# A patch-and-text Mamba layer with a shared and a routed FFN on one core: the four engines' work behind the last scan is put in another order

## The reference, cut to what matters

```python
h = concat([cls, patches(x) @ W + b], axis=1) + pos_enc         # 64 sequences
h = concat([h, txt], axis=1)                                    # 114 tokens of 256
h = h + mamba(layernorm(h))            # in-proj, conv, silu, selective scan, y * silu(z) @ W_out
def moe(v):                            # v = layernorm(h)
    sh  = ln(silu(v @ sw1.T + sb1) * (v @ sw2.T + sb2)) @ sw3.T + sb3
    xm  = v[index_b, index_t]                       # 512 chosen rows
    s   = sigmoid(xm @ [sg_w; eg_w].T + bias)       # 1 shared score, 8 expert scores
    top = argmax(s[:, 1:] + exp_bias);  w = softmax([s[:, 0], s[:, 1:][top]])
    z   = ln(silu(xm @ ew1 + eb1) * (xm @ ew2 + eb2))          # all 8 experts, hidden 128
    e   = (z @ ew3 + eb3)[top]
    sh[index_b, index_t] = sh[index_b, index_t] * w[0] + e * w[1]
    return sh
out = h + moe(layernorm(h))
```

## Time and profile before

| | before |
|---|---|
| median of three runs | 1710.02 us (1707.89 to 1710.78) |
| the profiled execution | 1707.03 us, of which the span is 1704.8 us |
| busy: PE, DVE, ACT, POOL | 87%, 90%, 78%, 92% of the span |
| last scan ends, last combine begins | 1619.58 us, 1700.00 us |
| granted TensorE clock over the span | 0.948 of full |

### The profile page before, as it was taken

The page is one execution under the profiler, slowest core; times in us unless marked ns, Lnnn a source line. Parts: engine busy times, 40 slices in busy tenths (PEclk is TensorE's granted clock), DMA queues, the critical chain, the costliest instruction groups (busy, mean ns, idle before and its releaser), DMA issues.

```text
span 1704.8 us, 27981 instructions
## 1 busy us (share of the span) xinstructions
PE 1485.8 (87%) x9868; PEld 1062.9 (62%) x9868; DVE 1539.9 (90%) x1360; ACT 1322.1 (78%) x3071; POOL 1562.6 (92%) x782
## 2 busy tenths in 40 slices
PE   7778898898998988988989889899898898987688
PEld 7555666666666666666666666666666666654355
DVE  2599999999999999999999999999999999998944
ACT  2577888888888888888888888888888888886644
POOL 0699999999999999999999999999999999999914
PEclk9898999999999999999999999999999999997799
DMA  5667665555666555556665555566655565656110
GB/s 142 141 135 183 166 139 124 125 128 132 147 131 148 136 123 125 131 131 145 133 148 134 125 123 132 133 144 133 148 134 123 124 132 133 139 125 140 40 35 16
DMA packets 194430, 218.47 MB, mean 128 GB/s; under 512 B 94011, under 2 KB 184773, under 8 KB 193778
## 3 DMA queue, kind: packets, MB, share of 16 engines
q1 hardware_dynamic: 193522, 215.51, 55.4%
q0 software_dynamic: 576, 1.17, 0.3%
q10 hardware_dynamic: 192, 0.01, 0.0%
HBM read 169.92 MB, written 47.09 MB: 127 GB/s over the span
## 4 chain that ended last, share of the span: by engine, by line
DVE 27%; POOL 25%; PE 16%; ACT 15%; issue 10%; DMA 5%; SPq 1%; DVEq 0%; ACTq 0%; POOLq 0%
POOL xr L1757 16%; DVE psum L1375 13%; ACT psum L1046 7%; DVE xr L1384 7%; DVE xr L1375 5%; POOL xr L1765 5%; PE psum L624 4%; POOL u L1778 3%; DMA u<-u_scratch 3%; PE psum L725 2%; ACT L1077 2%; PE psum L796 2%; ACT soft L1094 2%; PE psum L797 2%; ACT soft L1098 1%
## 5 line engine op out<-in xcount | busy, mean ns | idle before, releaser
L1757 POOL TENSOR_TENSOR xr<-u,bbc 128x912 f32<-128x912 f32 x512 | 1075.6, 2132 | 13.6 <-DMA u<-u_scratch 13.6
L1046 ACT ACTIVATE psum<-delta,a_neg 128x228 f32<-128x228 f32 x2048 | 804.9, 441 | 209.1 <-DVE xr L1384 178.8
L1375 DVE TENSOR_TENSOR_SCAN psum<-psum,xr 128x912 f32<-128x912 f32 x320 | 655.1, 2047 | 14.3 <-POOL xr L1757 8.4
L1765 POOL TENSOR_TENSOR xr<-xr,cbc 128x912 f32<-128x912 f32 x192 | 408.3, 2126 | 32.5 <-DVE xr L1375 32.3
L1375 DVE TENSOR_TENSOR_SCAN xr<-psum,xr 128x912 f32<-128x912 f32 x192 | 393.1, 2047 | 19.1 <-ACT psum L1046 19.1
L1384 DVE TENSOR_TENSOR xr<-psum,cbc 128x912 f32<-128x912 f32 x320 | 352.3, 1101 | 4.8
L725 PE MATMUL psum<-xr,fold 128*32 128x228 f32 x4096 | 297.4, 388 | 27.5 <-DVE xr L1384 14.7
L624 PE MATMUL psum<-xh,win 128*128 128x228 f32 x1024 | 220.3, 364 | 30.9 <-ACT xs L1077 24.9
L624 PEld LDWEIGHTS psum<-xh,win 128*128 128x128 f32 x1024 | 190.8, 191 | 57.4 <-ACT xs L1077 35.0
L675 PE MATMUL psum<-xi,conv_d 128*128 128x228 f32 x1024 | 211.4, 358 | 0.0
L675 PEld LDWEIGHTS psum<-xi,conv_d 128*128 128x128 f32 x1024 | 190.9, 189 | 16.4 <-issue 11.7
(11 more groups left out here) (207 smaller groups left out, 1550.1 us busy)
## 6 DMA issues: line engine op xcount, KB each, us to landing
delta<-delta_scratch SPq DMA_DIRECT2D x256, 228.0 KB, 6.6
u<-u_scratch SPq DMA_DIRECT2D x256, 228.0 KB, 4.3
bbc<-bc_scratch SPq DMA_DIRECT2D x128, 114.0 KB, 2.5
u_scratch<-u SPq DMA_DIRECT2D x64, 228.0 KB, 3.6
cbc<-bc_scratch SPq DMA_DIRECT2D x128, 114.0 KB, 2.7
delta_scratch<-delta SPq DMA_DIRECT2D x64, 226.0 KB, 5.6
out<-ob SPq DMA_DIRECT2D x32, 228.0 KB
h_scratch<-h SPq DMA_DIRECT2D x31, 228.0 KB
```

The source lines that it names most:

```text
L1046: ins = nc.scalar.activation(slot(k)[:, j * TOK:(j + 1) * TOK], delta4[:, c // 2, j, c % 2], ACT.Exp, scale=a_neg[:, c, j, n:n + 1])
L1375: nc.vector.tensor_tensor_scan(x if k in on_pool(i) else slot(k), slot(k), x, 0.0, ALU.mult, ALU.add).then_inc(scan_done, 1)
L1757: nc.gpsimd.tensor_tensor(xr[:, k % XRING], u4[:, c // 2, :, c % 2], bbc[:, p, n].unsqueeze(1).to_broadcast([P, J, TOK]), ALU.mult).then_i ...
L1765: nc.gpsimd.tensor_tensor(xr[:, k % XRING], xr[:, k % XRING], cbc[:, p, k % NI].unsqueeze(1).to_broadcast([P, J, TOK]), ALU.mult).then_inc ...
```

## The change

It touches the tail and the end of the body of group 31, and nothing before. (1) The last output projection is split: `out_first` (both identity parts and the first two of four wout chunks) stands in group 31's body, where bias_rows was; `out_second` (the other two chunks) opens the tail. Its PSUM bank is CB and no longer AB. (2) bias_rows moves into the tail and into bank 0. (3) The last FFN group uses bank BB and no longer 3, and its output leaves through xs and no longer through ob, so hidden(0, 1) waits for the copy of group 30 and not for that of 31. (4) All four engines' tails are written in another order. (5) SP no longer waits between the last two output DMAs.

```diff
-            h2_ps = psum[0:T, AB, 0:SEQ * DM].rearrange("p (s d) -> p s d", s=SEQ)
+            def h2_ps(g):
+                return psum[0:T, CB if g == GROUPS - 1 else AB, 0:SEQ * DM].rearrange("p (s d) -> p s d", s=SEQ)
+            def ob_of(g):
+                if g == GROUPS - 1:
+                    return xs[:, (GROUPS - 2) % 2].rearrange("p c t -> p (c t)")[:, 0:SEQ * DM].rearrange("p (s d) -> p s d", s=SEQ)
+                return ob[:]
...
-                return {GROUPS - 2: 2, GROUPS - 1: 3}.get(g, AB)
+                return {GROUPS - 2: 2, GROUPS - 1: BB}.get(g, AB)
...
-                        sp.dma_start(out_groups[g], ob[0:T]).then_inc(out_out, 16)
-                        sp.wait_ge(out_out, 16 * (g + 1))
+                        sp.dma_start(out_groups[g], ob_of(g)[0:T]).then_inc(out_out, 16)
...
+                    def out_first():
+                        g = GROUPS - 1
+                        pe.wait_ge(sz_done, 2 * GROUPS)
+                        pe.wait_ge(y_done, CH // 2 * g + 1)
+                        for s in range(SEQ):
+                            for k in range(DC):
+                                pe.matmul(h2_ps(g)[:, s, k * P:(k + 1) * P], h0[:, g % HRING, k, s * T:(s + 1) * T], ident[:],
+                                          start=(s == 0 and k == 0), stop=False)
+                            for c in range(CH // 2):
+                                pe.matmul(h2_ps(g)[:, s], y[:, g % 2, c, s * T:(s + 1) * T], wout[:, c], start=False, stop=False)
+                    def out_second():
+                        g = GROUPS - 1
+                        pe.wait_ge(y_done, CH // 2 * GROUPS)
+                        for s in range(SEQ):
+                            for c in range(CH // 2, CH):
+                                mm = pe.matmul(h2_ps(g)[:, s], y[:, g % 2, c, s * T:(s + 1) * T], wout[:, c],
+                                               start=False, stop=(s == SEQ - 1 and c == CH - 1))
+                        mm.then_inc(h2_mm, 1)
...
+                        if runs(i):
+                            reduce_states(i, 13)
                         if i == GROUPS - 1:
-                            bias_rows()
-                        if runs(i):
-                            reduce_states(i, 13)
+                            out_first()
...
                     def hidden(m, j):
+                        pe.wait_ge(xmt_ev, m + 1)
                         if m >= 1:
                             pe.wait_ge(a_done, 2 * m - 1 + j)
                         elif j == 0:
-                            pe.wait_ge(scan_done, UNITS * GROUPS)
-                            pe.wait_ge(c_dve, ALL_DVE)
+                            pe.wait_ge(eb3_done, 1)
                         else:
-                            pe.wait_ge(o_done, GROUPS)
+                            pe.wait_ge(o_done, GROUPS - 1)
...
                     def out_copy(g):
                         act.wait_ge(f3_mm, g + 1)
-                        need(act, out_out, 16 * g)
-                        nc.scalar.activation(ob[0:T], f3_ps(g), ACT.Copy).then_inc(o_done, 1)
+                        if g == GROUPS - 1:
+                            act.wait_ge(h2_mm, GROUPS)
+                        else:
+                            need(act, out_out, 16 * g)
+                        nc.scalar.activation(ob_of(g)[0:T], f3_ps(g), ACT.Copy).then_inc(o_done, 1)
...
-                    turn_out(0)
                     hidden(3, 0)
+                    turn_out(0)
                     hidden(3, 1)
-                    for m in range(1, MT):
-                        turn_out(m)
-                        expert_out(m - 1)
-                    expert_out(MT - 1)
+                    turn_out(1)
+                    expert_out(0)
+                    turn_out(2)
+                    expert_out(1)
+                    expert_out(2)
+                    turn_out(3)
+                    expert_out(3)
```

More of the change, by code:

```diff
@@ L997, in expert_out @@
                         mm.then_inc(e3_mm, 1)
-                    pe.wait_ge(gw_in, GW_IN)
-                    v_center(ga)
-                    h2_turn(gz)
-                    v_var(ga)
-                    ffn_in(gz)
+                    out_second()
+                    v_center(GROUPS - 3)
+                    h2_turn(GROUPS - 2)
+                    v_var(GROUPS - 3)
+                    ffn_in(GROUPS - 2)
+                    bias_rows()
+                    v_center(GROUPS - 2)
+                    h2_turn(GROUPS - 1)
+                    ffn_out(GROUPS - 3)
+                    v_var(GROUPS - 2)
                     turn_rows(0)
-                    ffn_out(ga)
-                    v_center(gz)
+                    ffn_in(GROUPS - 1)
                     turn_rows(1)
                     hidden(0, 0)
-                    v_var(gz)
                     turn_rows(2)
+                    ffn_out(GROUPS - 2)
                     turn_rows(3)
-                    ffn_out(gz)
-                    for m in range(MT):
-                        gates(m)
+                    gates(0)
+                    gates(1)
+                    gates(2)
+                    v_center(GROUPS - 1)
+                    gates(3)
                     hidden(0, 1)
+                    v_var(GROUPS - 1)
                     hidden(1, 0)
@@ new lines, in gate_weights, with hot_copy @@
+                    def gate_weights():
+                        act.wait_ge(gate_step, GATE_STEPS - 3)
+                        nc.scalar.activation(wts[:], two[:], ACT.Exp).then_inc(gate_act, 1)
+                    def hot_copy():
+                        act.wait_ge(hot_mm, 1)
+                        nc.scalar.activation(hot_t.rearrange("p m t -> p (m t)"), psum[0:E, CB, :], ACT.Copy).then_inc(hot_ev, 1)
+                    ln2_rstd(GROUPS - 2)
+                    h2_scale(GROUPS - 2)
+                    h2_copy(GROUPS - 1)
@@ L1351, in _ @@
[L1351 to L1352 removed]
+                    out_copy(GROUPS - 2)
+                    gate_scores()
+                    v_square(GROUPS - 1)
+                    ln3_rstd(GROUPS - 1)
+                    gate_weights()
                     gate_silu(0)
[L1354 to L1355 removed]
@@ L1356, in _ @@
                     gate_silu(1)
+                    out_copy(GROUPS - 1)
                     affine(0)
+                    hot_copy()
                     gate_silu(2)
+                    affine(1)
                     zt_copy(0)
-                    affine(1)
                     gate_silu(3)
-                    for m in range(1, MT):
-                        zt_copy(m)
-                        if m + 1 < MT:
-                            affine(m + 1)
+                    affine(2)
+                    zt_copy(1)
@@ L1367, in _ @@
+                    zt_copy(2)
+                    affine(3)
+                    zt_copy(3)
                 @block.vector
@@ L1544, in body @@
                             scan(i, 15)
-                        if runs(i - 2) and not in_window(i - 2):
+                        if i < GROUPS - 1 and runs(i - 2) and not in_window(i - 2):
                             ffn_first(i - 2)
```

204 lines of the change are left out of this document (100 added, 104 removed).

## The result

The changed kernel has a median of 1699.98 us over five runs (1697.99 to 1701.16), the kernel before 1710.01 us over five runs beside them (1707.89 to 1710.78). The ratio is 0.9942, with an interval from 0.9929 to 0.9954: 10.0 us less.

The account below looks back on a forecast made before the run. The prediction took a latency chain, then PE's queue, to bound the tail. Head 4.2 us and second part 1.1 us shorter made 5.3 us less, a median of 1704.7 us (-0.31%), range 1700.5 to 1708.5.

Parts of the forecast that it names:

- the old tail's price (61.4): PE's time from the first turn_rows to the last expert_out's end in the old profile: 61.4 us, 56.74 busy.
- the rival of the clock: PE's granted clock falls in the new, denser tail: slower, 2.5 to 7.5 us lost, up to 1712; chance 0.05.
- the head: Latency chain from the last scan's end to turn_rows(0): 4.2 us shorter, turn_rows(0) at most 14.7 us behind the scan.
- the second part: PE's queue from turn_rows(0) to the end: 61.4 us before, 60.25 after, 1.1 us shorter.
- The stall of turn_out(2): PE's wait for affine(2), behind POOL's rstd_of(2) and shared_rows: keeps its old 1.16 us, bounds 0.3 and 2.4.
- the larger-gain rival: The head's gain is larger and the meeting at POOL falls away: 6.1 us less, 1703.9; chance 0.15.
- The three terms: Head's gain: 2.7 us from the split projection, 1.0 from ACT's order, 0.45 from DVE's order at the first tile.
- Cost nothing: out_first's eight matmuls, 2.7 us, take bias_rows's old place; the last two units' reductions come no later.
- expert_out(3): New stall at the end: it waits for zt_copy(3), covered only by a bias matmul; 0.6 us with hand-overs.
- turn_hot: New meeting point needing the choice's end: PE has 7.3 us of work, the choice takes 5.9; cover 1.4, cost nothing.
- The output of group 31: Its DMA must land before POOL's shared_rows; hidden, with some 3 us to spare.
- The collision of gated: gated(3) on DVE beside a POOL step, 1.06 us instead of 0.20; in the new order 0.86 us should be saved.

Follow-up runs that it names:

- before_again: Unchanged copy of the kernel before, run for its profile: 1709.02 us, ratio 1.0003.
- before_3: Another unchanged copy of the kernel before, run for its profile: 1709.34 us, ratio 0.9997.
- before_4: A further unchanged copy of the kernel before, run for its profile: 1707.65 us, ratio 0.9994.
- after_again: Unchanged copy of the changed kernel, run for its profile: 1699.39 us, ratio 0.9943 to the kernel before.
- after_3: Another unchanged copy of the changed kernel, run for its profile: 1699.72 us, ratio 0.9948 to the kernel before.
- after_4: A further unchanged copy of the changed kernel, run for its profile: 1700.26 us, ratio 0.9949 to the kernel before.
- before_warm: The kernel before with 16 spare, unread matmuls of 128x128 in group 31's body, ahead of the reductions: 1708.86 us, ratio 1.0002.
- the three filled profiles: The kernel before with 8, 8 and 4 spare matmuls ahead of ffn_out(29), hidden(1, 0) and turn_out(2), run three times: 1707.88, 1707.55, 1706.72 us.
- late_bias: The changed kernel with bias_of(0, 0) behind the whole choice again, ahead of bias_of(0, 1): 1705.71 us, ratio 0.9977 to the kernel before.
- turn3_first: The changed kernel with turn_out(3) ahead of expert_out(2), as in the kernel before: 1704.78 us, ratio 0.9975 to the kernel before.
- unsplit: The changed kernel with the whole last projection in the tail, out_first directly ahead of out_second: 1704.12 us, ratio 0.9968 to the kernel before.

## Why the gain was larger than forecast

All eight profiles of the two kernels, in us behind the last scan's end; "low clock" are the groups that ran at the 1.2 GHz level from out_first or ffn_out(29) on.

| | turn_rows(0) | from there to the last combine | last combine | low clock |
|---|---|---|---|---|
| before, first | 18.94 | 61.48 | 80.42 | none |
| before_again | 19.12 | 63.15 | 82.27 | expert_out(1) |
| before_3 | 20.40 | 63.51 | 83.91 | ffn_out(29), hidden(1, 0) |
| before_4 | 20.43 | 62.08 | 82.51 | ffn_out(29) |
| mean | 19.72 | 62.56 | 82.28 | |
| after, first | 16.14 | 58.25 | 74.39 | out_first |
| after_again | 16.13 | 58.14 | 74.27 | out_first |
| after_3 | 14.80 | 58.20 | 73.00 | none |
| after_4 | 16.24 | 58.20 | 74.44 | out_first |
| mean | 15.83 | 58.20 | 74.03 | |

**The step that failed** is the sentence "before, 2.28 and 2.29 us of it did not lower the clock". (The stretch in rows 8 begins at 1638.5, behind the 2.28 us stall; the full clock behind both is in that trace.) It held for one execution, and both the old tail's price (61.4) and the rival of the clock were read from that one. In three of four profiles of the kernel before at least one of its stalls was followed by a group at the low clock: 5.38 for 3.72, 5.32 for 3.70, and ffn_out(29) with rows of 1.06 for 0.60. before_warm, which has the same code from the last scan on, shows it at ffn_out(29) too (last combine at 82.24), and none of the three filled profiles has it.

Against its own first profile the mean of the four is 0.8 us longer in the head and 1.1 in the second part, 1.9 in all. The clock makes some 1.5 of it: 1.66 and 1.62 in the two slow groups of the second part, and about 1.3 in the head of before_3 and of before_4, over four profiles. Of the rest 0.2 is turn_out(2), which waits 1.38 or 1.39 us in three of them and not 1.16, since the POOL step that meets gated(3) took 1.28 us there and 1.06 in the first profile.

The mechanism of the rival was right, with the wrong sign: it is the kernel before that pays, since it has the stalls. No profile of the changed kernel shows a low clock behind out_first, and filling (1.2 us gained, and no low clock left) and adding stalls (4.9 us for one of 3.27, and 3.0 on top of one of 2.71) both show that it is the stalls. The mechanism is tested from both sides; its share, about 1.5 us, rests on four profiles. That the forecast of the pair came out within 0.7 us (6.0 against 5.3) is luck: there the errors of head and second part nearly cancel.

**The second part**, forecast 1.1 us shorter, was 3.2 in the pair and 4.4 in the means. Three terms make 3.1 of the missing 3.3: the executions of before with slow groups (1.1, as above), the idle time ahead of turn_out(2), and the busy time.

The stall of turn_out(2), which "stays" at 1.16 with a lower bound of 0.3, is all but gone. The first gather of shared_rows begins 30.3 us behind turn_rows(0) (1666.27 - 1635.95), where it began 33.8 behind it (1672.27 - 1638.52): 3.4 us earlier, because bias_of(0, 0) no longer waits for the choice (in late_bias, where it waits again, the gather begins 34.5 us behind, 1.6 of it from the low clock). The four gathers are 0.4 us shorter (5.47 us to L1918, before 5.91), and L1923 took 0.20 us where L1866 took 1.06, since no gated runs beside it. Together 4.7 us, and affine(2) ends at 1677.54, 1.1 us ahead of turn_out(2). But now turn_out(2) waits for zt_copy(1), which stands behind affine(2) on ACT and ends at 1678.53. The profile names no such wait, but the rows show it. Here are zt_copy(1) on ScalarE's timeline, and the weight loads of turn_out(2) on that of PEld:

```profile
1677.44 1.09 ACT L1341 ACTIVATE xr<-psum,selg 128x1024 f32<-128x1024 f32 x1
...
1678.65 0.86 PEld L1001 LDWEIGHTS psum<-ident,xr 128*128 128x128 f32 x8 [0.36 <-issue]
```

turn_out(2) follows the start of expert_out(0) after 3.71 us, and after 3.56 in late_bias, where zt_copy(1) ends 0.7 us ahead of it: 0.15 us are paid. So what turn_out(2) waits for came 3.7 us forward and PE 2.5. The difference is the 0.86 of the POOL step and the 0.4 of the gathers. "Both chain and PE move forward by nearly the same" was right but for these, and the larger-gain rival was right that the meeting falls away. Without that the stall would have stayed at about 1.0 us (an estimate: 0.15 + 0.86). No run tests this by itself.

The last term, 0.8, is that a stall was priced too low: 56.74 busy before and 1.65 for ffn_in(31) make 58.39, and 57.56 were busy. Rows of one queue overlap (a hidden of 3.68 us is followed by its successor after 3.52 where nothing holds it up). A stall takes that overlap away on top of its idle time, and the first row behind it is up to 0.09 us longer: about 0.5 us over the three stalls, and 0.3 not traced.

**The head**, forecast 4.2, was 2.8 in the pair and 3.9 in the means. The three terms are right where the clock is full: after_3 has turn_rows(0) at 14.80 for the forecast 14.7, h2_copy at +4.77 where it was +7.57, and ACT and DVE follow at once. Wrong was "Cost nothing" for out_first. With the 2.34 us wait for POOL ahead of it, PE does the reductions ahead of it and its first half at the low clock (0.67 in the stretch), the last reductions come later, y comes at +3.4 instead of +2.1, and 1.3 us are lost, in three of four profiles. It is the clock and not the place. late_bias has the same head, and the reductions ahead of out_first begin 2.8 us before the last scan's end as in the first profile of after. But the wait for POOL is short there, the clock is full, and y comes at +2.08. TensorE's timeline of late_bias:

```profile
1621.65 0.98 PE L732 MATMUL psum<-xr,fold 128*32 128x228 f32 x16 [0.71 <-POOL xr L1822]
1622.56 0.69 PE L760 MATMUL psum<-ident,h 128*114 128x128 f32 x4
```

turn3_first, again with the same head, has the full clock as well (turn_rows(0) at 14.82), so it is three of six, and by these six the head's mean is 15.5 and not 15.8. bias_rows cost nothing, as said: turn_rows(0) waited 0.19 us for DVE, not for PE. The split by itself was forecast at 2.7 us: between unsplit and after_3 h2_copy's start and turn_rows(0) both move by 3.24 us, because the whole projection is partly done at the low clock too.

**The other steps.** expert_out(3) waits 0.58 us, forecast 0.6. turn_hot never waits. The output of group 31 landed in time. The collision of gated did not vanish but moved: L1724 took 3.08 us from 1674.91 beside POOL's subtraction from 1674.55 to 1676.91, where it takes 1.23 alone. It ends 1.1 us behind the subtraction, so it did little beside it. This agrees with the lock that the prediction cites from the Trainium skill. It costs nothing only because turn_out(3) now stands behind expert_out(2); with the old order of these two it is most of the 2.71 us stall of turn3_first (gated(3) took 3.18 us there, 1.95 more than alone), which the forecast did not see.

**The sum.** The forecast was 2.9 us short of what the tails of the means show (8.25 against 5.3): 1.9 for the slow executions of before, 1.2 for turn_out(2) and 0.8 for what a stall costs, less 1.1 in the head after, nearly all of it out_first. These tails differ by 8.25 us, the times by 9.0 (with the first comparison's five runs on each side: 1708.96 over 143 runs, 1699.92 over 21, give or take 0.8). The 0.8 left are within what these can tell, and the six heads of above would take 0.3 of them. The main part, which is the same code in both, adds scatter: the last scan ended between 1617.83 and 1620.23 before and between 1618.74 and 1624.76 after; after_4's profile, with a span of 1704.0, has the latest of these ends and a tail like the others'. The first comparison's 10.0 us and the 9.0 of all runs differ by no more than such scatter.

No version tried beats the changed kernel.

## What to carry to other kernels

A stall of TensorE in a dense stretch costs more than its idle time: the overlap with its successor each time, and in some executions 1.6 us or more for work at the low clock behind it; price it from several profiles, and look at where the profiled execution stands among the runs. Work that nobody waits for is best put where such a stall stands. When an order is changed, follow every condition of a meeting point by its own start: a wait that holds a collision in it (1.06 us for a step of 0.20) is not a fixed price, and a condition that is met early can have another close behind it (affine(2) and zt_copy(1) here).

## What the runs showed of the hardware

The granted clock fell behind idle stretches of only 1.39 us (before_again), 2.28 (before_3, before_4) and 2.34 us (the changed kernel's head), and in other executions of the same code it did not: 2.28 and 2.29 us in the first profile of before are followed by 1.00. The 1.39 us of before_3, and the 1.11 us ahead of the fourth turn_rows in every profile of before, are followed by the full clock. The Trainium skill (TensorE: Matmul & The Clock Gate, Part 1) calls the warm-up ramp "run-variable". By that, one execution doesn't give the price, and these traces agree, for a fall in the middle of a kernel. The mean clock of the span tells little of it: 0.948 for the first profile of before and for before_4, which has a slow group, and 0.944 for before_3.
